# A token mixer, masked attention product and routed FFN on one Trainium2 core: x rows of tile 3 loaded earlier, attention weights split in halves of 512, prologue order rewritten

## Chip, cores and metric

The kernel runs on one core of one Trainium2 chip. The metric is the device time of one execution in microseconds (us). Three timed executions of the kernel before gave 526.52, 526.66 and 527.02 us (median 526.66). The profiled execution is another one, with a time of its own.

## What is computed

The input `x` is (16, 128, 64, 2): 16 channels c, 128 heads h, 64 complex states n. The output is (16, 128, 1024).

```python
# 1. token mixer (S4D): K[c,h,l] = Re( sum_n W'[c,h,n] * exp(dt_Lambda[h,n] * l) ),  l = 0..1023
dt_Lambda = exp(log_dt) * Lambda
W' = W * (exp(dt_Lambda) - 1) * reciprocal((exp(dt_Lambda * 1024) - 1) * Lambda)
h = einsum('chn,hnl->chl', W', exp(dt_Lambda * pos)).real
# 2. attention product with a block mask (32 x 32 blocks, kept where the mask's sum is over 0)
h = h + layernorm(h) @ (weight * block_mask).T          # weight 1024 x 1024
# 3. FFN with a sparsemax router over 8 experts of rank 16
y = layernorm(h)
h = h + y @ W_base.T + b_base + sum_e sparsemax(y @ W_router.T + b_router)[e] * (y @ lora_A[e]) @ lora_B[e]
```

## The kernel before

The 16 x 128 = 2048 rows of length 1024 are worked on in 16 tiles of 128 rows (8 heads x 16 channels). For each tile `t`:

- ScalarE and VectorE build two small tables (`sines`, `exponentials`, `phases`, `decay_b`, `v_factors`), VectorE multiplies them with x into `v_sb` (`table_v`), and `b_sb` is built on GpSimd in the prologue and on VectorE in the loop (`table_b`). TensorE multiplies the two per head (`k_transposed`), which gives K transposed in `turnp`.
- `k_high` (ScalarE) and `k_low` (VectorE) split it into a high and a low fp32r part, the stationary operand of the attention product. `k_turn` (VectorE) turns it back; SyncE stores it to `rows_out` in four transfers and loads it again as rows `h1` (`k_rows`), of which `k_sum` and `k_deviation` take the statistics.
- `attention(t, k)`, k = 0..7, is the product with the attention weights, in three passes (high x high, low weights, low data) over both halves of 512 columns: 6 matmuls a chunk. `attention_residual` scales it and adds `h1`.
- `h2_transposes`, `h2_high`, `h2_low` prepare the FFN's operand; `lora_router` gives expert activations and logits, `gates` the sparsemax, `gated_transpose`/`gated_high`/`gated_low` their split operand, `base(t, k)` the base product, `experts` the expert product, `result` the output rows; GpSimd's `add_bias` prepares the rows that `result` adds to.

The rows of x come into one buffer `xn`, which `load_x(t)` (SyncE) fills and `x_rows_twice(t)` (ScalarE) copies to `xd`; `x_transposes(t)` (TensorE) turns it into the PSUM bank `xps` that `table_v(t)` reads. There is one `xn` and one `xps`, so `load_x(t)` waits for `x_rows_twice(t-1)`, that one for `x_transposes(t-1)`, and `x_transposes(t)` for `table_v(t-1)`.

The loop over tiles 2 to 15 has two products per step: attention of tile t, base of tile t-1. Ahead of it stands a **prologue**, an order of calls written out by hand on each engine, in which tiles 0 to 3 start and the weights are prepared:

- Attention weights, 8 row blocks j: `mask_sums(j)` (VectorE) and `block_sums(j)` (TensorE) give the block mask, `wa_mask(j)` (VectorE) applies it, `wa_centre(j)` (ScalarE for j < 6, GpSimd for 6 and 7) takes the row's mean off, `wa_transposes(j)` (TensorE) transposes it in two halves i = 2j, 2j+1 of 512 columns into the two halves of `acc_b`, `wa_copies(j)` (ScalarE) rounds them to `wa_hi`, and `wa_lo` is the difference: from PSUM by VectorE (`wa_lows`), or for j = 1, 3, 5 (`BY_POOL`) by GpSimd from a copy in SBUF that `wa_copies(j)` makes as well. A half of `acc_b` is used again when both have read it.
- Base weights, 16 halves i: `wb_half(i)` (TensorE), `wb_highs(i)` (ScalarE), `wb_lows(i)` (VectorE), through the same two halves of `acc_b`.
- `first_attention(n, [k])` is the attention product of tile 0, first for the half n = 0 of the columns (weights j = 0..3), then for n = 1.
- `q_arguments`, `q_tanh`, `q_sines`, `reciprocal_of_tanh`, GpSimd's `parameters` and `reciprocal_of_norm` give the factor of W': round 0 for the heads of tiles 0 and 1, round 1 for all others.

The product of tile 0 (base and experts) closes the prologue: `base(0, 0)` waits for all 16 `wb_high` and `wb_low`, `gated_transpose(0)` for `gates(0, 0)`, `experts()` for `gated_low(0)`.

Each engine works through its own list in order. SyncE's list is: all mask and attention weight rows, `load_x(1)`, base weights, LoRA A, `load_x(2)`, `k_rows(0)`, `k_rows(1)`, a wait for `q_ready` 2 (the end of `parameters(1)`), LoRA B (into `lb_raw`), the bias, `load_x(3)`, `k_rows(2)`, `load_x(4)`. The waits of its `k_rows` are:

```python
sp.wait_ge(kt_turned, t + 1)                 # k_turn(t)
if at(t, 1):
    sp.wait_ge(h2_ready, t)                  # attention_residual(0, 0)
...                                          # four stores to rows_out
sp.wait_ge(k_out, (t + 1) * 16 * Q)          # they have landed
```

Of the kernel before, what the change touches and what calls it, by code (L numbers as in the profile page):

```python
# [21 lines left out]
P = 128  # L22
# [47 lines left out]
def build_vit_tower(nc, x, log_dt, lam, w_attn, mask, w_base, b_base, w_router, b_router, lora_a, lora_b,  # L70
# [4 lines left out]
    with ExitStack() as ctx:  # L75
# [138 lines left out]
        def half_bank(i):  # L214
            return acc_b[:, (i % 2) * HALF:(i % 2 + 1) * HALF]
# [91 lines left out]
        def _(sp):  # L307
# [28 lines left out]
            k_rows(0)  # L336
            k_rows(1)
# [3 lines left out]
            load_x(3)  # L341
# [26 lines left out]
        def _(pe):  # L368
# [16 lines left out]
            def wa_transposes(j):  # L385
                if j < CENTRE_LAST:
                    pe.wait_ge(wa_centred, j + 1)
                else:
                    pe.wait_ge(wa_centred_last, j + 1 - CENTRE_LAST)
                for i in (2 * j, 2 * j + 1):  # L390
                    if i >= 2:
                        pe.wait_ge(wa_high, i - 1)
                        if (i - 2) // 2 in BY_POOL:
                            pe.wait_ge(wa_copied, raws(i - 1))
                        else:
                            pe.wait_ge(wa_low_direct, i - 1 - raws(i - 1))
# [146 lines left out]
            block_sums(7)
            pe.wait_ge(kt_lo, 1)
            wa_rows_ready(NWT // 2)
            first_attention(0, [0])
            wa_transposes(4)
# [3 lines left out]
            x_transposes(1)  # L551
            wa_transposes(5)
            wa_transposes(6)
            wa_transposes(7)
            first_attention(0, [4])
            first_attention(0, [5])
            first_attention(0, [6])
            wb_half(0)
            wb_half(1)
            first_attention(0, [7])  # L560
# [55 lines left out]
            experts()  # L616

# [20 lines left out]
        def _(act):  # L638
# [129 lines left out]

            q_tanh(0)
            q_sines(0)  # L770
            sines(0)
            wa_centre(0)
            exponentials(0)
            wa_centre(1)
            wa_centre(2)
            wa_copies(0)
            x_rows_twice(0)
# [589 lines left out]
```

## Time and profile before

| | before |
|---|---|
| timed executions | 526.66 us median (526.52 to 527.02) |
| profiled execution, its time | 525.62 us |
| profiled execution, its span (first to last instruction) | 523.8 us |
| mean granted TensorE clock | 0.984 |
| busy in the span: PE, PEld, DVE, ACT, POOL | 92%, 78%, 78%, 50%, 23% |
| `experts()` of tile 0 ends, the loop's first instruction starts | 110.5 us |

PE is TensorE's matmul, PEld its weight load, DVE VectorE, ACT ScalarE, POOL GpSimd, SP SyncE. All times of the trace are counted from the start of the span. The part ahead of 110.5 us is the prologue; the rest are the 14 steps of the loop and the tail.

### The profile page before, as it was taken

Reading aid. Unit: us, or ns where it says so; the run is one execution under the profiler, and the core shown is the slowest. Engines: PE = TensorE matmul, PEld = TensorE weight load, DVE = VectorE, ACT = ScalarE, POOL = GpSimd, SP = SyncE. Lnnn points to the kernel's source line nnn. Section 1 sums busy time; section 2 is a strip of 40 time slices with the busy share of each in tenths; the row PEclk is TensorE's granted clock in tenths of the full one; section 3 lists DMA queues with packets and bytes.
Section 4 is the critical chain, followed back from the end, with each engine's and each line's share of the span. In section 5 each row is a group of like instructions: output and inputs, shape, how many; then the busy total and the mean of one; then the engine's idle time right before and its main releaser. Section 6 shows DMA issues by size and latency. Waiting matters only on the chain.

```text
span 523.8 us, 7437 instructions
## 1 busy us (share of the span) xinstructions
PE 480.9 (92%) x2467; PEld 407.9 (78%) x2467; DVE 410.9 (78%) x866; ACT 262.4 (50%) x477; POOL 122.1 (23%) x106
## 2 busy tenths in 40 slices
PE   0548977989999999999999999999999999999995
PEld 0446766878888888888888888888888888888884
DVE  7998985998988889888888878887889888854241
ACT  2687976467363636455464646362635446232200
POOL 0574694440201103030303030201203030303020
PEclk9997988999999999999999999999999999999998
DMA  8994113031312121221203040312121120303011
GB/s 286 403 320 68 37 42 126 1 94 37 92 37 81 44 80 45 49 76 40 85 8 117 0 111 14 90 35 80 45 80 47 42 79 18 103 20 102 1 40 40
DMA packets 28764, 40.83 MB, mean 78 GB/s; under 512 B 10760, under 2 KB 21192, under 8 KB 28744
## 3 DMA queue, kind: packets, MB, share of 16 engines
q1 hardware_dynamic: 28368, 40.49, 25.5%
q8 instruction: 10, 0.16, 0.1%
q10 hardware_dynamic: 376, 0.10, 0.1%
q14 instruction: 10, 0.08, 0.0%
HBM read 23.80 MB, written 16.78 MB: 77 GB/s over the span
## 4 chain that ended last, share of the span: by engine, by line
PE 83%; ACT 5%; DVE 4%; POOL 3%; DMA 3%; issue 1%; SPq 0%; DVEq 0%; POOLq 0%
PE acc_b L455 36%; PE acc_a L455 31%; PE turnp L439 5%; PE small L479 4%; PE turnp L448 3%; DMA xn<-in_x 2%; PE small L481 1%; PE acc_b L399 1%; ACT wa_hi L661 1%; ACT wa_raw L655 1%; ACT wb_hi L670 1%; PE xps L429 1%; POOL wr L937 0%; ACT wa_raw L664 0%; PE acc_b L420 0%
## 5 line engine op out<-in xcount | busy, mean ns | idle before, releaser
L946 POOL TENSOR_TENSOR h<-h,st 128x1024 f32<-128x1024 f32 x16 | 30.3, 1894 | 328.6 <-PE turnp L448 321.5
L455 PE MATMUL acc_a<-wa_hi,x_hi 128*128 128x512 f32 x256 | 84.2, 405 | 2.1 <-POOL wa_lo L925 1.6
L455 PE MATMUL acc_b<-wb_hi,x_hi 128*128 128x512 f32 x256 | 83.9, 404 | 0.0
L455 PE MATMUL acc_a<-wa_lo,x_hi 128*128 128x512 f32 x256 | 81.4, 394 | 0.0
L455 PE MATMUL acc_a<-wa_hi,x_lo 128*128 128x512 f32 x256 | 81.0, 393 | 0.0
L455 PE MATMUL acc_b<-wb_lo,x_hi 128*128 128x512 f32 x256 | 80.6, 391 | 0.0
L455 PE MATMUL acc_b<-wb_hi,x_lo 128*128 128x512 f32 x256 | 80.5, 391 | 0.0
L455 PEld LDWEIGHTS acc_a<-wa_lo,x_hi 128*128 128x128 f32 x256 | 48.9, 191 | 10.2
L455 PEld LDWEIGHTS acc_a<-wa_hi,x_lo 128*128 128x128 f32 x256 | 48.5, 190 | 10.4
L742 ACT ACTIVATE x_hi<-turnp 128x1024 fp32r<-128x1024 f32 x16 | 16.4, 1023 | 80.0 <-PE turnp L448 80.0
L455 PEld LDWEIGHTS acc_a<-wa_hi,x_hi 128*128 128x128 f32 x256 | 47.7, 192 | 11.0 <-DVE x_lo L1150 1.7
L455 PEld LDWEIGHTS acc_b<-wb_hi,x_lo 128*128 128x128 f32 x256 | 48.1, 188 | 10.4
L455 PEld LDWEIGHTS acc_b<-wb_lo,x_hi 128*128 128x128 f32 x256 | 48.1, 188 | 10.3
L455 PEld LDWEIGHTS acc_b<-wb_hi,x_hi 128*128 128x128 f32 x256 | 44.9, 189 | 8.2
L1216 DVE SCALAR_TENSOR_TENSOR h<-acc_b,st,h 128x1024 f32<-128x1024 f32 (+1 forms) x17 | 20.7, 1220 | 25.5 <-PE acc_b L455 25.5
L949 POOL TENSOR_TENSOR h<-h,bias 128x1024 f32<-128x1024 f32 x16 | 39.4, 2465 | 1.3
L748 ACT ACTIVATE hw_hi<-small 128x128 fp32r<-128x128 f32 x16 | 4.4, 278 | 64.6 <-PE small L487 64.6
L1150 DVE TENSOR_TENSOR x_lo<-turnp,x_hi 128x1024 fp32r<-128x1024 f32 x16 | 19.6, 1224 | 21.9 <-ACT x_hi L707 21.9
L439 PEld LDWEIGHTS turnp<-v_sb,b_sb 128*128 128x128 f32 x256 | 31.3, 195 | 1.8 <-issue 0.8
L479 PE MATMUL small<-wr,x_hi 128*128 128x272 f32 x128 | 32.1, 338 | 0.0
L439 PE MATMUL turnp<-v_sb,b_sb 128*128 128x128 f32 x256 | 31.9, 279 | 0.2 <-issue 0.2
L682 ACT ACTIVATE er_t<-er_t 128x256 f32<-128x256 f32 x15 | 6.3, 418 | 48.4 <-DVE er_t L1073 48.4
(200 smaller groups left out, 940.2 us busy)
## 6 DMA issues: line engine op xcount, KB each, us to landing
h<-rows_out SPq DMA_DIRECT2D x16, 512.0 KB, 3.3
out<-h SPq DMA_DIRECT2D x15, 512.0 KB
rows_out<-b_sb SPq DMA_DIRECT2D x56, 128.0 KB, 2.3
mask_raw<-in_L_attn_mask SPq DMA_DIRECT2D x8, 512.0 KB, 10.0
wa_raw<-in_L_attn_weight SPq DMA_DIRECT2D x8, 512.0 KB, 10.7
wb_raw<-in_L_ffn_W_base SPq DMA_DIRECT2D x8, 512.0 KB, 8.8
rows_out<-tmp SPq DMA_DIRECT2D x8, 128.0 KB, 2.3
xn<-in_x SPq DMA_DIRECT2D x15, 64.0 KB
```

The source lines that it names most:

```text
L399: mm = pe.transpose(half_bank(i)[:, k * P:(k + 1) * P], every_eighth, ident)
L429: mm = pe.transpose(xps[:, r * P:(r + 1) * P], xd[:, r, :, :].rearrange("p d n -> p (d n)"), ident)
L439: mm = pe.matmul(kt_pairs[:, h // HG, :, h % HG * C:(h % HG + 1) * C], b_sb[:, h, :, :].rearrange("p x y -> p (x y)"), v_sb[:, h, :, :], s ...
L448: mm = pe.transpose(turnp[:, k * P:(k + 1) * P], h2[par][:, k * P:(k + 1) * P], ident)
L455: return pe.matmul(cols, a, rows, start=first, stop=last)
L479: pe.matmul(small[:, 0:2 * CAT], x_hi[:, k, :], wr[:, k, :, :].rearrange("p s n -> p (s n)"), start=k == 0, stop=False)
L682: act.activation(er_of(t), er_of(t), ACT.Exp).then_inc(tab_exp, 1)
L742: act.activation(x2_of(t)[0][:, :, :].rearrange("p k n -> p (k n)"), turnp[:, :], ACT.Copy)\
L946: pool.tensor_tensor(h2[par][:, :], h2[par][:, :], st2[:, par, 1:2].to_broadcast([P, L]), ALU.subtract)\
L949: pool.tensor_tensor(h2[par][:, :], h2[par][:, :], bias[:, :], ALU.add).then_inc(bias_added, 1)
L1150: dve.tensor_tensor(by_pair(lo), kt_pairs, by_pair(hi).bitcast(F), ALU.subtract).then_inc(kt_lo, 1)
L1216: dve.scalar_tensor_tensor(h, acc_b[:, cols], st2[:, par, 4:5], h, ALU.mult, ALU.add).then_inc(out_ready, 1)
```

## The change

1. SyncE: `load_x(3)` moves up, from behind LoRA B and the bias to right behind `k_rows(0)`.
2. `wa_transposes(j)` and `wa_copies(j)`, which did both halves of a block, become `wa_half(i)` (TensorE), `wa_highs(i)` and `wa_raws(j)` (ScalarE), and `wa_lows` of VectorE takes a half i. The waits of each half are as before. `wa_raws(j)` stands behind both `wa_highs` of its block.
3. The lists of TensorE, ScalarE and VectorE in the prologue are in another order; the instructions are the same ones. GpSimd's list is unchanged. The tables of numbers that follow the calls (which tile, which half) are unchanged.

```diff
             k_rows(0)
+            load_x(3)
             k_rows(1)
             sp.wait_ge(q_ready, len(ROUNDS))
             sp.dma_start(lb_raw[:, :], lora_b.rearrange("e r l -> (e r) l")).then_inc(lorb_in, 16)
             sp.dma_start(bias[:, :], b_base.partition_broadcast(P)).then_inc(bias_in, 16)
-            load_x(3)
             k_rows(2)
             load_x(4)
...
-            def wa_transposes(j):
+            def wa_half(i):
+                j = i // 2
                 if j < CENTRE_LAST:
                     pe.wait_ge(wa_centred, j + 1)
                 else:
                     pe.wait_ge(wa_centred_last, j + 1 - CENTRE_LAST)
...
-            def wa_copies(j):
-
+            def wa_highs(i):
+
+                act.wait_ge(wa_t, i + 1)
+                act.activation(half_of(wa_hi, i), half_bank(i), ACT.Copy).then_inc(wa_high, 1)
+
+            def wa_raws(j):
+
+                act.wait_ge(wa_t, 2 * j + 2)
                 for i in (2 * j, 2 * j + 1):
-                    act.wait_ge(wa_t, i + 1)
-                    act.activation(half_of(wa_hi, i), half_bank(i), ACT.Copy).then_inc(wa_high, 1)
-                if j in BY_POOL:
-                    for i in (2 * j, 2 * j + 1):
-                        act.activation(raw_half(i), half_bank(i), ACT.Copy).then_inc(wa_copied, 1)
+                    act.activation(raw_half(i), half_bank(i), ACT.Copy).then_inc(wa_copied, 1)
...
-            def wa_lows(j):
-
-                dve.wait_ge(wa_t, 2 * j + 2)
-                for i in (2 * j, 2 * j + 1):
-                    dve.wait_ge(wa_high, i + 1)
-                    dve.tensor_tensor(half_of(wa_lo, i), half_bank(i), half_of(wa_hi, i).bitcast(F), ALU.subtract)\
-                        .then_inc(wa_low_direct, 1)
+            def wa_lows(i):
+
+                dve.wait_ge(wa_t, i // 2 * 2 + 2)
+                dve.wait_ge(wa_high, i + 1)
+                dve.tensor_tensor(half_of(wa_lo, i), half_bank(i), half_of(wa_hi, i).bitcast(F), ALU.subtract)\
+                    .then_inc(wa_low_direct, 1)
```

The lists after the change, by calls (TensorE, from the fourth block sum on; ScalarE and VectorE where the prediction speaks of them; `hi`/`lo`/`raw` are `wa_highs`, `wa_lows`, `wa_raws`):

```
TensorE: wa_half 0,1 | router transpose | block_sums 3,4 | x_transposes 0 | block_sums 5 | wa_half 2,3,4,5 |
  block_sums 6 | k_transposed 0 | wa_half 6 | x_transposes 1 | wa_half 7 | block_sums 7 | wa_half 8,9 |
  first_attention 0: k 0-3 | wa_half 10-15 | first_attention 0: k 4-7 | wb_half 0,1 | first_attention 1: k 0-4 |
  wb_half 2,3 | k 5 | x_transposes 2 | k_transposed 1 | k 6,7 | wb_half 4-9 | attention(1,0) |
  h2_transposes 0 | attention(1,1) | wb_half 10,11 | attention(1,2),(1,3) | wb_half 12,13 |
  attention(1,4),(1,5) | wb_half 14,15 | lora_router 0 | attention(1,6),(1,7) | k_transposed 2 |
  base(0,0) to (0,6) | gated_transpose 0 | base(0,7) | experts | x_transposes 3
ScalarE: ... exponentials 0 | centre 2 | hi 2,3 | raw 1 | centre 3,4 | x_rows_twice 1 | hi 4,5,6 | k_high 0 |
  hi 7 | raw 3 | hi 8,9 | exponentials 1 | centre 5 | sines 1 | hi 10,11 | raw 5 | x_rows_twice 2 |
  hi 12-15 | q_tanh 1 | wb_highs 0,1 | k_sum 0, k_deviation 0 | wb_highs 2,3 | router/LoRA copy | q_sines 1 |
  wb_highs 4 | k_high 1 | ... | wb_highs 10,11 | sines 2 | k_sum 1 | wb_highs 12-15 | x_rows_twice 3 |
  k_deviation 1 | exponentials 3 | k_high 2 | h2_centre 1 | LoRA B copy | gated_high 0 | sines 3
VectorE: ... lo 4,5 | phases 1 | wa_mask 5,6 | k_low 0 | wa_mask 7 | lo 8,9 | router_columns |
  q_arguments 1 | decay_b 1 | k_turn 0 | lo 12,13 | v_factors 1 | lo 14,15 | table_v 1 | wb_lows 0,1 | ... |
  wb_lows 10,11 | h2_reciprocal 0 | v_factors 2 | decay_b 2 | wb_lows 12,13 | table_v 2 | wb_lows 14,15 |
  h1_reciprocal 1 | attention_residual 1 | phases 3 | gates 0 | k_low 2 | k_turn 2 | gated_low 0 |
  result 0 | v_factors 3 | table_v 3
```

Three places, row by row. SyncE, behind the rows of tile 0 (L319 and L322 are the rows of K of one tile, L311 is `load_x`):

```order
 L319 DMA rows_out<-tmp 32x4x256 x4
 L322 DMA h<-rows_out 128x1024
+L311 DMA xn<-in_x 128x1x128
 L319 DMA rows_out<-tmp 32x4x256 x4
 L322 DMA h<-rows_out 128x1024
-L339 DMA lb_raw<-in_L_ffn_lora_B 128x1024
-L340 DMA bias<-in_L_ffn_b_base 128x1024
-L311 DMA xn<-in_x 128x1x128
+L340 DMA lb_raw<-in_L_ffn_lora_B 128x1024
+L341 DMA bias<-in_L_ffn_b_base 128x1024
```

The load of the x rows passes the rows of tile 1 and the two loads that wait for `parameters(1)`.

VectorE around `k_low(0)` (L1150), before: `wa_mask(5)` and `wa_mask(6)` (L1044) stand on either side of it, then round 1 of the arguments (L1013 to L1018) and the two lows of block 4 (L1052):

```order
L1044 SCALAR_TENSOR_TENSOR wa_raw,wa_sum<-acc_a,wa_raw 128x1024
L1150 TENSOR_TENSOR x_lo<-turnp,x_hi 128x4x8x32
L1044 SCALAR_TENSOR_TENSOR wa_raw,wa_sum<-small,wa_raw 128x1024
```

The same place after the change (L1170 is `k_low(0)`, L1065 `wa_mask`, L1072 the lows of halves 8 and 9):

```order
L1065 SCALAR_TENSOR_TENSOR wa_raw,wa_sum<-acc_a,wa_raw 128x1024
L1065 SCALAR_TENSOR_TENSOR wa_raw,wa_sum<-small,wa_raw 128x1024
L1170 TENSOR_TENSOR x_lo<-turnp,x_hi 128x4x8x32
L1065 SCALAR_TENSOR_TENSOR wa_raw,wa_sum<-acc_a,wa_raw 128x1024
L1072 TENSOR_TENSOR wa_lo<-acc_b,wa_hi 128x512 x2
```

`wa_mask(6)` now stands ahead of `k_low(0)`, and `wa_mask(7)` and block 4 right behind it.

VectorE behind the gates of tile 0, before: `k_low(2)` (L1150), `gated_low(0)` (L1210), `k_turn(2)` (L1156), `v_factors(3)` (L1094 to L1100), `result(0, 0)` (L1216):

```order
L1150 TENSOR_TENSOR x_lo<-turnp,x_hi 128x4x8x32
L1210 TENSOR_TENSOR hw_lo<-small,hw_hi 128x128
L1156 STREAM_TRANSPOSE b_sb<-turnp 128x4x8x32
L1094 TENSOR_TENSOR xy<-xy,er_t 128x128
L1096 TENSOR_TENSOR t<-xy,qr 128x128
L1097 TENSOR_TENSOR t<-xy,qi 128x128
L1099 TENSOR_TENSOR u<-t 128x64
L1100 TENSOR_TENSOR u<-t 128x64
L1216 SCALAR_TENSOR_TENSOR h_0<-acc_b,st,h_0 128x1024
```

The same after the change, with the line numbers of the changed kernel (L1176 is `k_turn(2)`, L1230 `gated_low(0)`, L1236 `result(0, 0)`):

```order
L1170 TENSOR_TENSOR x_lo<-turnp,x_hi 128x4x8x32
L1176 STREAM_TRANSPOSE b_sb<-turnp 128x4x8x32
L1230 TENSOR_TENSOR hw_lo<-small,hw_hi 128x128
L1236 SCALAR_TENSOR_TENSOR h_0<-acc_b,st,h_0 128x1024
L1114 TENSOR_TENSOR xy<-xy,er_t 128x128
```

`k_turn(2)` has passed `gated_low(0)`, and `v_factors(3)` follows `result(0, 0)`.

## Rows read from the trace of the kernel before

**Rows 1.** By stretch: length, busy PE, PEld, DVE, ACT, POOL, granted clock, DMA share, GB/s

```profile
26.00:39.00 13.00, 6.18 (x38) 5.63 (x37) 12.86 (x20) 11.03 (x23) 9.37 (x5) 1.00 0.99 325
...
78.00:91.00 13.00, 9.44 (x50) 8.15 (x49) 7.47 (x16) 7.88 (x19) 6.62 (x5) 0.87 0.36 127
...
140.00:523.00 383.00, 377.88 (x1938) 320.45 (x1936) 289.30 (x622) 173.18 (x315) 60.12 (x28) 1.00 0.20 57
```

**Rows 2.** Waits between 0 and 112 us: in total, times, longest

```profile
PE acc_b L420 <- ACT wb_hi L670: 3.6, 1, 3.6
...
PE small L487 <- DVE hw_sb L1197: 1.8, 1, 1.8
```

**Rows 3.** Timeline of SyncE's queue: start us, us, engine line op

```profile
78.46 0.35 SPq L339 DMA_DIRECT2D lb_raw<-in_L_ffn_lora_B  x1
...
79.34 0.64 SPq L311 DMA_DIRECT2D xn<-in_x  x1
```

**Rows 4.** Timeline of ScalarE: start us, us, ..., [idle before <-releaser]

```profile
35.49 1.11 ACT L664 ACTIVATE wa_raw<-acc_b 128x512 f32<-128x512 f32 x2
...
85.31 0.52 ACT L677 ACTIVATE xd<-xn 128x128 f32<-128x128 f32 x2 [5.02 <-DMA xn<-in_x]
```

**Rows 5.** Timeline of TensorE

```profile
39.28 0.77 PE L455 MATMUL acc_a<-wa_hi,x_hi 128*128 128x512 f32 x1 [1.57 <-POOL wa_lo L925]
...
74.34 1.04 PE L448 MATMUL turnp<-kst,h 128*128 128x128 f32 x8
...
87.14 1.94 PE L420 MATMUL acc_b<-kst,wb_raw 128*128 128x128 f32 x8 [3.56 <-ACT wb_hi L670]
...
96.00 0.71 PE L455 MATMUL acc_b<-wb_hi,x_hi 128*128 128x512 f32 x2
...
101.53 0.62 PE L455 MATMUL acc_b<-wb_hi,x_hi 128*128 128x512 f32 x2
...
122.65 2.02 PE L439 MATMUL turnp<-v_sb,b_sb 128*128 128x128 f32 x16 [0.18 <-issue]
```

**Rows 6.** Timeline of VectorE in the prologue

```profile
37.09 1.22 DVE L1150 TENSOR_TENSOR x_lo<-turnp,x_hi 128x1024 fp32r<-128x1024 f32 x1
38.23 1.22 DVE L1044 SCALAR_TENSOR_TENSOR wa_raw<-small,wa_raw 128x1024 f32<-128x1024 f32 x1
...
62.37 2.13 DVE L1168 TENSOR_TENSOR st<-st 128x1 f32<-128x1 f32 x1
...
93.89 1.28 DVE L1174 SCALAR_TENSOR_TENSOR h<-acc_a,st,h 128x1024 f32<-128x1024 f32 x1 [0.70 <-issue]
...
99.43 2.17 DVE L1191 TENSOR_TENSOR gate<-gate,gs 128x64 f32<-128x64 f32 x1
...
103.63 2.21 DVE L1196 TENSOR_SCALAR gs<-gs,tau 128x8 f32<-128x8 f32 x1
105.87 0.29 DVE L1197 TENSOR_TENSOR hw_sb<-cat,gs 128x128 f32<-128x128 f32 x1
...
107.41 2.19 DVE L1156 STREAM_TRANSPOSE b_sb<-turnp 128x1024 f32<-128x1024 f32 x1
```

**Rows 7.** VectorE in the first step of the loop, the same gate operation

```profile
131.18 0.22 DVE L1191 TENSOR_TENSOR gate<-gate,gs 128x64 f32<-128x64 f32 x1
```

**Rows 8.** Timeline of GpSimd in the prologue

```profile
36.67 2.35 POOL L925 TENSOR_TENSOR wa_lo<-wa_raw,wa_hi 128x1024 fp32r<-128x1024 f32 x1 [3.55 <-ACT wa_raw L664]
...
61.95 2.53 POOL L937 TENSOR_TENSOR wr<-wr_raw,wr 128x1088 fp32r<-128x1088 f32 x1 [4.20 <-ACT wr L806]
...
86.25 2.37 POOL L912 TENSOR_TENSOR b_sb<-b_sb,h 128x1024 f32<-128x1024 f32 x1
99.12 2.40 POOL L941 TENSOR_TENSOR lb_lo<-lb_raw,lb_hi 128x1024 fp32r<-128x1024 f32 x1 [10.51 <-ACT lb_hi L831]
101.48 1.89 POOL L946 TENSOR_TENSOR h<-h,st 128x1024 f32<-128x1024 f32 x1
103.45 2.36 POOL L949 TENSOR_TENSOR h<-h,bias 128x1024 f32<-128x1024 f32 x1
```

More of the change, by code:

```diff
@@ L550, in _ @@
             first_attention(0, [3])
[L551 to L554, printed above, removed]
+            wa_half(10)
+            wa_half(11)
+            wa_half(12)
+            wa_half(13)
+            wa_half(14)
+            wa_half(15)
             first_attention(0, [4])
@@ L589, in _ @@
             attention(1, 3)
+            wb_half(12)
+            wb_half(13)
+            attention(1, 4)
+            attention(1, 5)
+            wb_half(14)
+            wb_half(15)
             pe.wait_ge(h2t_lo, 1)
@@ L616, in _ @@
             experts()
+            x_transposes(3)
             steps(pe, step)
@@ L767, in _ @@
             act.dma_start(rt_stage, w_router.rearrange("e (k p) -> (e k) p", p=P)).then_inc(rt_in, 16)
+            x_rows_twice(0)
             q_tanh(0)
[L770 to L777, printed above, removed]
-            wa_centre(3)
-            x_rows_twice(1)
             act.wait_ge(ldt_in, 16)
@@ L782, in _ @@
             act.wait_ge(consts_in, 16)
-            wa_copies(1)
+            q_sines(0)
+            wa_centre(0)
+            wa_centre(1)
+            sines(0)
+            wa_highs(0)
+            wa_highs(1)
+            exponentials(0)
+            wa_centre(2)
+            wa_highs(2)
+            wa_highs(3)
+            wa_raws(1)
+            wa_centre(3)
             wa_centre(4)
-            wa_copies(2)
+            x_rows_twice(1)
+            wa_highs(4)
+            wa_highs(5)
+            wa_highs(6)
             k_high(0)
-            wa_copies(3)
+            wa_highs(7)
+            wa_raws(3)
+            wa_highs(8)
+            wa_highs(9)
+            exponentials(1)
+            wa_centre(5)
             sines(1)
-            exponentials(1)
-            wa_copies(4)
-            wa_centre(5)
-            wa_copies(5)
+            wa_highs(10)
+            wa_highs(11)
+            wa_raws(5)
             x_rows_twice(2)
+            wa_highs(12)
+            wa_highs(13)
+            wa_highs(14)
+            wa_highs(15)
             q_tanh(1)
-            wa_copies(6)
-            wa_copies(7)
-            q_sines(1)
             wb_highs(0)
@@ L806, in _ @@
             act.activation(wr[:, :, 0, :], cat_raw, ACT.Copy).then_inc(cat_hi, 1)
+            q_sines(1)
+            wb_highs(4)
             k_high(1)
-            wb_highs(4)
             wb_highs(5)
@@ L812, in _ @@
             wb_highs(7)
+            h2_centre(0, 0)
             wb_highs(8)
             wb_highs(9)
-            h2_centre(0, 0)
             h2_deviation(0, 0)
             h2_high(0)
+            wb_highs(10)
+            wb_highs(11)
             sines(2)
-            wb_highs(10)
-            x_rows_twice(3)
-            wb_highs(11)
+            k_sum(1)
             wb_highs(12)
-            k_sum(1)
-            k_deviation(1)
             wb_highs(13)
@@ L827, in _ @@
             wb_highs(15)
+            x_rows_twice(3)
+            k_deviation(1)
             exponentials(3)
+            k_high(2)
             h2_centre(1, 1)
@@ L1328, in _ @@
             k_low(2)
+            k_turn(2)
             gated_low(0)
-            k_turn(2)
-            v_factors(3)
             dve.wait_ge(ffn_ready, 1)
             result(0, 0)
+            v_factors(3)
             table_v(3)
```

122 lines of the change are left out of this document (62 added, 60 removed).

## Prediction

> **What bounds the kernel now.** I read the granted clock and the busy time by stretch first. In the loop TensorE is busy 377.9 of 383 us at full clock, so only the prologue and the first step can give anything [rows 1]. The prologue falls in two parts. From 26 to 39 us VectorE works 12.86 of 13 us while TensorE works 6.18: this part is bound by VectorE's list, and TensorE's first attention product starts at 39.28, right behind `k_low(0)` (37.09 plus 1.14) and GpSimd's `wa_lo` of block 3, which ends at 39.03 [rows 1, 5, 6, 8]. From 78 to 91 us TensorE is busy 9.44 of 13 us, at a mean clock of 0.87 of full speed, and nobody else is full: that is waiting, not work [rows 1].
>
> The wait that ends last there is in ScalarE's timeline: `x_rows_twice(3)` stands idle 5.02 us until 85.31 for the x rows of tile 3 [rows 4]. SyncE issued them at 79.34, behind LoRA B at 78.46, which waits for the end of `parameters(1)` [rows 3]. Behind it on ScalarE is `wb_highs(11)`, and TensorE's `wb_half(13)` starts at 87.14 after 3.56 us of idle, eight transposes in 1.94 us where eight of `h2_transposes` took 1.04 [rows 2, 5]. The half-speed stretch is the 1.2 GHz level, after the idle. The other end of this part is the gates of tile 0, for which TensorE waits 1.8 us [rows 2]. The prologue closes at 110.5 us.
>
> **Part by part.** No instruction is added or taken away, so I followed each list with the durations of the rows. A VectorE pass over 128x1024 costs 1.14 us from start to start [rows 6], a half of 512 0.6 on VectorE and 0.5 on ScalarE, an attention or base chunk of six matmuls 1.38 at full clock (from 96.00 to 101.53 there are four) [rows 5]. The results:
>
> *Up to the first attention: later by 1.9 us.* VectorE has `wa_mask(6)` ahead of `k_low(0)`, 1.14 us [rows 6], and two short waits of 0.5 (for GpSimd's norm) and 0.8 (for `wa_highs(4)`, which now stands behind `wa_centre(3)`, `(4)` and `x_rows_twice(1)`); 0.25 of idle goes. `k_low(0)` ends at 40.5 instead of 38.3. ScalarE's raw copies of block 3 end at 38.7 instead of 36.6 [rows 4], so GpSimd's `wa_lo`, 2.35 us, ends at 41.1 instead of 39.0 [rows 8]. TensorE starts at 41.2 instead of 39.3.
>
> *41 to 76 us: about level.* What TensorE lacks there it has done before: `wa_half(8)` and `(9)`, 1.9 us at half clock, no longer stand among the chunks. `wa_mask(7)` is done 5 us earlier, which takes the late centring by GpSimd off the path of blocks 6 and 7. VectorE finishes `table_v(1)` at about 56.2, as before, `k_turn(0)` 1.2 later. Then `h1` lands 1.2 us later, ScalarE's `k_deviation(0)` ends about 1.0 later, and `q_sines(1)` with its table load (1.97 us) is now behind it instead of ahead. The wait in front of `wb_half(6)` stays. I get the end of `h2_transposes(0)` at 75.9 against 75.2 to 75.4 before [rows 5].
>
> One collision I can't place: VectorE's first operation of `reciprocal_of_tanh(1)` would start at 62.9, GpSimd's `cat_lo` at about the same moment. In the trace a 128x1 operation of VectorE that began with this GpSimd operation in progress (61.95, 2.53 us) took 2.13 us, from 62.37 until that was over [rows 6, 8]. If GpSimd is first, `wb_lows(4)` is 1.7 us late and 1.1 us of it reach the end; if not, nothing. Between 0 and 1.1 I take 0.5.
>
> *76 us to the end of attention: earlier by 4.9 us.* The x load now goes out right behind the rows of tile 0, near 53 us, when `x_rows_twice(2)` is done; even 6 us of transfer end 25 us before `x_rows_twice(3)`. So the 5.02 and the 3.56 us go, and with them the half-clock transposes (0.9) and chunks (about 0.7) behind them. In their place TensorE's list runs nearly closed: 75.9, plus `wb_half(10..13)` 1.8, four chunks 5.5, `wb_half(14,15)` 1.2 with a short wait, `lora_router` 1.85, two chunks 2.75. Attention of tile 1 ends at 88.9; before it was 93.8, since `attention_residual(1,1)` starts at 93.89 [rows 6]. `k_transposed(2)` adds 1.8, and base starts at 90.7 instead of 96.0 [rows 5]. What is late next is GpSimd: `parameters(1)` starts at 65.5 instead of 64.5 and takes 14.0 us, then `v_factors(2)`, `decay_b(2)` and 6.2 us of `table_b(2)` end at 88.8, against 88.6 before [rows 8]. It gave 5 us of slack before and gives none now: a further gain ahead of this point is worth nothing.
>
> *From there to the gates: 0.4 later.* The gates' end stood 12.3 us behind the end of attention (105.87 plus 0.29 against 93.8) [rows 6]. Three gate operations are stretched by the three GpSimd operations beside them, among them one of 2.17 us that takes 0.22 in the loop; they end as those end [rows 6 to 8]. Their start comes from ScalarE's copy of LoRA B, and `k_high(2)` now stands ahead of it. I take the same distance plus 0.4: 101.7.
>
> *Gates to the end of `experts`: 0.65 later.* Before, TensorE's own chunks filled the time behind the gates: 110.5 minus 106.15 is 4.35. Now `gated_low(0)` stands behind `k_low(2)` (1.14) and `k_turn(2)` (2.19) [rows 6], 0.3 more for itself, and the expert product 1.36: 5.0. TensorE arrives at `gated_transpose(0)` near 100.3, and has only `base(0,7)` to fill 3.6 us: a new wait of about 2 us at `experts`.
>
> *First step: 0.4 later.* `k_transposed(3)` waits 0.18 us at 122.65, so VectorE's chain to `table_b(3)` is already even with TensorE [rows 5]. `v_factors(3)`, 1.2 us, is now inside that chain, behind `result(0, 0)`, which in turn starts 0.6 earlier relative to the end of experts; `x_transposes(3)` (0.2) moves from one place of TensorE's list to another. Net 0.4. Behind it the loop has slack on VectorE (289 of 383 us) [rows 1].
>
> The sum: -4.9 + 0.4 + 0.65 + 0.4 + 0.5 = -2.95 us. Of the profiled execution's 525.6 us that leaves 522.7. The median of the runs shown is 1.0 us above that execution, so I forecast 523.7 us.
>
> **Rivals.** *Forecast case* (the x wait goes, the new waits at `experts` and in the first step take part of it): gain 1.2 to 4.8, chance 0.60.
>
> *The gates slip through*, gain 5.2, 521.5 us, chance 0.18. The first stretched operation (99.43) began 0.3 us after GpSimd's (99.12) [rows 6, 8]; by my times it now begins 0.4 us before, and is done. Then only two are held, and the gates end at 99.5 instead of 101.7. Against it: the last gate operation would then stand beside GpSimd's third one, and rows show it only after that was over. The Trainium skill (SBUF — State Buffer, "Who interferes with whom") says that a VectorE instruction with two SBUF inputs contends with a GpSimd one that reads SBUF, and that the loser waits for the whole instruction; by that rule the last operation, both of whose inputs are in SBUF, is held too and the end is 101.7 again. The trace agrees on the first of them: 2.17 against 0.22 us.
>
> *The late start stays*, gain 1.0, 525.7 us: no change, chance 0.13. The 1.9 us at the first attention aren't made up by the work done ahead, because TensorE meets new waits at `wa_half(12)` and `(14)` (ScalarE's `sines(1)`, 3.3 us with its table load, stands ahead of `wa_highs(10)`). -2.95 + 1.9 = -1.05. The same result stands for the case that the x rows were hidden after all. For it: the walk rests on a dozen near ties; against it: VectorE's list, which binds, has no new work.
>
> *GpSimd's parameter chain becomes the path*, slower, 528.7 us, chance 0.09. `q_sines(1)` is behind `k_deviation(0)` and the router copy, so `parameters(1)` moves with `h1`, which moves with `k_turn(0)`. Each us that it starts behind 65.5 is one us at `k_transposed(2)`, at `attention_residual(1,1)` and at the gates. The kernel turns slower when it starts 3 us later, behind 68.5; at 70.5 (`h1` landing late, and the collision at 62.9 delaying what the chain waits for) it is -2.95 + 5 = +2.05. Against it: GpSimd is free from 58 us on, and the rows of `h1` have the DMA engines nearly alone.
>
> **How the numbers follow.** A measurement of this kernel can tell about 0.2% (1.05 us) from no change. Faster by more: 0.60 + 0.18 = 0.78; within it 0.13; slower 0.09. The range takes the forecast case, the slipping gates with 2 us of error on my walk, and the late start: 519.2 to 526.2.
>
> **What would show it.** Right: `x_rows_twice(3)` without idle; base of tile 0 starting near 90.7; first attention near 41.2; idle of about 2 us in front of the expert product; `table_b(2)` of GpSimd ending within 0.5 us of `k_transposed(2)`; 0.5 us of idle at `k_transposed(3)`. Wrong: base starting later than 94, `parameters(1)` starting after 68, or a first attention that starts as early as before.

## The result, and the profile after

Over eight runs of each, the changed kernel takes 525.21 us (median; 524.42 to 525.60), the kernel before 526.84 us (526.10 to 527.62). The ratio is 0.9968 [0.9957, 0.9978]: 1.6 us faster, half of the 3.1 us that the forecast of 523.7 us meant.

| | before | after |
|---|---|---|
| median us | 526.84 | 525.21 |
| profiled execution / span, us | 525.62 / 523.8 | 524.96 / 523.1 |
| VectorE, ScalarE, GpSimd busy, after | | 411.4 (79%), 262.8 (50%), 122.0 (23%) |

The two profiled executions differ by only 0.7 us, because before's lies 1.2 us below its median and after's 0.25 below. The windows of the kernel after answer to [rows 1] (length, busy PE, PEld, DVE, ACT, POOL, granted clock, DMA share, GB/s):

```profile
26.00:39.00 13.00, 9.51 (x48) 9.00 (x49) 12.11 (x21) 9.02 (x17) 6.93 (x4) 0.98 0.98 321
65.00:78.00 13.00, 8.66 (x37) 7.00 (x37) 10.70 (x14) 10.40 (x16) 12.02 (x25) 0.74 0.17 42
78.00:91.00 13.00, 12.93 (x77) 10.91 (x75) 11.01 (x24) 11.09 (x23) 7.11 (x6) 1.00 0.36 122
...
140.00:523.00 383.00, 377.21 (x1934) 319.72 (x1932) 288.83 (x622) 173.26 (x315) 59.69 (x28) 1.00 0.20 56
```

The hole between 78 and 91 us is closed: TensorE works 12.93 us of 13 at full clock, where it worked 9.44. The loop is as it was. The stretch ahead of the hole has become worse: 8.66 us of work at a granted clock of 0.74, where the same window of the kernel before reads

```profile
65.00:78.00 13.00, 9.82 (x52) 8.26 (x53) 11.66 (x16) 9.59 (x15) 11.94 (x25) 0.87 0.17 42
```

TensorE's timeline of the kernel after answers to [rows 5]:

```profile
41.66 0.77 PE L455 MATMUL acc_a<-wa_hi,x_hi 128*128 128x512 f32 x1 [0.64 <-ACT wa_hi L668]
...
67.57 0.63 PE L420 MATMUL acc_b<-kst,wb_raw 128*128 128x128 f32 x4 [2.52 <-ACT wb_hi L680]
69.37 1.08 PE L420 MATMUL acc_b<-kst,wb_raw 128*128 128x128 f32 x4 [1.17 <-ACT wb_hi L680]
71.10 1.94 PE L420 MATMUL acc_b<-kst,wb_raw 128*128 128x128 f32 x8 [0.64 <-ACT wb_hi L680]
...
75.40 1.40 PE L448 MATMUL turnp<-kst,h 128*128 128x128 f32 x8
...
90.72 0.61 PE L455 MATMUL acc_a<-wa_hi,x_lo 128*128 128x512 f32 x2
92.11 2.02 PE L439 MATMUL turnp<-v_sb,b_sb 128*128 128x128 f32 x16 [0.77 <-issue]
93.89 0.70 PE L455 MATMUL acc_b<-wb_hi,x_hi 128*128 128x512 f32 x2
...
105.62 0.70 PE L455 MATMUL acc_b<-lb_hi,hw_hi 128*128 128x512 f32 x2 [0.42 <-DVE hw_lo L1230]
107.08 0.38 PE L429 MATMUL xps<-kst,xd 128*128 128x128 f32 x2
...
121.98 2.02 PE L439 MATMUL turnp<-v_sb,b_sb 128*128 128x128 f32 x16 [2.76 <-issue]
```

The reader sees four things: the first attention product at 41.66; three waits ahead of `wb_half(6)` to `(8)`, with transposes at half clock behind them (eight in 1.94 us, granted clock 0.50); the base product of tile 0 at 93.89, only 2.1 us earlier than before; and a new wait of 2.76 us for `k_transposed(3)` in the first step, where 0.18 stood. ScalarE's row that answers to [rows 4] has no idle:

```profile
87.23 0.53 ACT L687 ACTIVATE xd<-xn 128x128 f32<-128x128 f32 x2
```

VectorE's timeline of the kernel after, where [rows 6] were read:

```profile
63.24 2.10 DVE L1045 TENSOR_SCALAR lb_raw<-bias 128x224 f32<-128x224 f32 x1
...
92.16 1.28 DVE L1194 SCALAR_TENSOR_TENSOR h<-acc_a,st,h 128x1024 f32<-128x1024 f32 x1
...
97.07 0.22 DVE L1211 TENSOR_TENSOR gate<-gate,gs 128x64 f32<-128x64 f32 x1
...
97.64 2.28 DVE L1214 SCALAR_TENSOR_TENSOR gs<-gs 128x8 f32<-128x8 f32 x1
...
100.16 1.63 DVE L1216 TENSOR_SCALAR gs<-gs,tau 128x8 f32<-128x8 f32 x1
101.82 0.29 DVE L1217 TENSOR_TENSOR hw_sb<-cat,gs 128x128 f32<-128x128 f32 x1
...
112.21 3.42 DVE L1144 TENSOR_TENSOR v_sb<-tmp,v_sb 128x1024 f32<-128x1024 f32 x1
```

And GpSimd's, where [rows 8] were read:

```profile
62.69 2.52 POOL L958 TENSOR_TENSOR wr<-wr_raw,wr 128x1088 fp32r<-128x1088 f32 x1 [3.73 <-ACT wr L826]
...
84.85 1.94 POOL L930 TENSOR_TENSOR b_sb<-pp,qq 128x1024 f32<-128x1024 f32 x1 [5.74 <-DVE qq L1152]
...
88.76 3.25 POOL L933 TENSOR_TENSOR b_sb<-b_sb,h 128x1024 f32<-128x1024 f32 x1
...
97.50 2.40 POOL L962 TENSOR_TENSOR lb_lo<-lb_raw,lb_hi 128x1024 fp32r<-128x1024 f32 x1 [5.49 <-ACT lb_hi L853]
99.86 1.90 POOL L967 TENSOR_TENSOR h<-h,st 128x1024 f32<-128x1024 f32 x1
101.84 2.54 POOL L970 TENSOR_TENSOR h<-h,bias 128x1024 f32<-128x1024 f32 x1
...
112.15 2.40 POOL L970 TENSOR_TENSOR h<-h,bias 128x1024 f32<-128x1024 f32 x1
```

Read in pairs. At 62.69 GpSimd's `cat_lo` begins, and VectorE's first operation of `reciprocal_of_tanh(1)` (63.24) is not done before it ends, at 65.2. The kernel before has a hold of the same length beside the same GpSimd operation, at a neighbouring operation of VectorE (62.37, 2.13 us [rows 6]). At 112.15 `add_bias(1)`'s second operation begins, 0.06 us ahead of the last operation of `table_v(3)` (L1144), which then takes 3.42 us instead of 1.23. In the kernel before the same pair stood the other way round: VectorE's began at 114.85 and took 1.23, GpSimd's at 114.88 and took 3.47.

So most of the time won by the end of the experts (their end, read as the start of `x_transposes(3)`: 107.08 against 110.52, 3.4 us) is gone at `k_transposed(3)` (121.98 against 122.65, 0.7 us).

### The profile page after: what moved, and what is told of

The parts are those of the page before. It is cut to its first block, busy times and chain, and to the rows that moved or that the text cites. A ratio compares the mean times of both kernels' runs of the same rounds, so it can differ in the third digit from the quotient of the medians.

```text
span 523.1 us, 7442 instructions
## 1 busy us (share of the span) xinstructions
PE 482.6 (92%) x2467; PEld 408.1 (78%) x2467; DVE 411.4 (79%) x866; ACT 262.8 (50%) x477; POOL 122.0 (23%) x106
## 4 chain that ended last, share of the span: by engine, by line
PE 84%; DVE 7%; ACT 3%; issue 3%; POOL 1%; DMA 0%; DVEq 0%; POOLq 0%; ACTq 0%
PE acc_b L455 36%; PE acc_a L455 32%; PE turnp L439 5%; PE small L479 4%; PE turnp L448 3%; PE small L481 1%; PE acc_b L420 1%; PE acc_b L399 1%; ACT wa_hi L668 1%; ACT wb_hi L680 1%; PE xps L429 1%; DVE wa_lo L1072 0%; DVE wb_lo L1078 0%; DVE gs L1214 0%; DVE mask_sum L1056 0%
## 5 line engine op out<-in xcount | busy, mean ns | idle before, releaser
L1236 DVE SCALAR_TENSOR_TENSOR h<-acc_b,st,h 128x1024 f32<-128x1024 f32 (+1 forms) x17 | 20.7, 1221 | 27.3 <-PE acc_b L455 27.3
L1170 DVE TENSOR_TENSOR x_lo<-turnp,x_hi 128x1024 fp32r<-128x1024 f32 x16 | 19.6, 1224 | 22.0 <-ACT x_hi L717 22.0
```

What stands on the lines that cost most here:

```text
L1170: dve.tensor_tensor(by_pair(lo), kt_pairs, by_pair(hi).bitcast(F), ALU.subtract).then_inc(kt_lo, 1)
L1236: dve.scalar_tensor_tensor(h, acc_b[:, cols], st2[:, par, 4:5], h, ALU.mult, ALU.add).then_inc(out_ready, 1)
```

## The experiments

Each kernel was timed over five rounds; medians of before measured beside it are given as (before ...). The comparison of the traces left two theories on the x load: that it brings about 4 us and the new order gives them back (`b1_x_alone`), and that the new order has made it worthless (`a1_x_late`).

**The x load alone taken back, and the x load alone.** `a1_x_late` is the changed kernel with

```diff
             k_rows(0)
-            load_x(3)
...
+            load_x(3)
             k_rows(2)
```

behind LoRA B and the bias, and `b1_x_alone` the kernel before with the opposite edit.

> The changed kernel with load_x(3) put back behind the bias, all else as changed. Theory (the new order has made the early load worthless): x_rows_twice(3) now stands behind wb_highs(15), at 87.2 us in the changed kernel's trace; a load issued at 80.0 lands near 86, so ScalarE waits for nothing, and the time is that of the changed kernel, 525.2 us within 0.5. Rival (my prediction's step: the load is what took the 5 us wait away): the wait comes back, at least 3 us slower than the changed kernel, 528 us.

> The kernel before with load_x(3) moved up behind k_rows(0), nothing else. Theory (the early load is the gain, the rest of the new order costs): x_rows_twice(3) starts at about 80.3 instead of 85.3, base of tile 0 near 91 instead of 96.0, then bound by GpSimd's table_b(2), which ends at 88.6; 4 to 5 us faster than before, about 522 us, faster than the whole change. Rival (the gain is capped by GpSimd's chain and by TensorE's waits as in the changed kernel): base starts near 94 and the gain is 1.5 us, 525.2 us.

`a1_x_late`: 525.31 us (before 527.12), 0.9971 [0.9958, 0.9984], the same as the changed kernel. Its SyncE and ScalarE, one row of each:

```profile
78.92 0.64 SPq L311 DMA_DIRECT2D xn<-in_x  x1
...
85.97 0.52 ACT L687 ACTIVATE xd<-xn 128x128 f32<-128x128 f32 x2
```

The rows are issued as late as before (78.92 against 79.34) and nobody waits for them: in the new order of ScalarE `x_rows_twice(3)` stands behind `sines(2)`, `k_sum(1)` and `wb_highs(12..15)`, and 7 us have passed. The early load is worth nothing beside the new order, as the recorded theory of this run had it.

`b1_x_alone`: 526.23 us (before 527.12), 0.9982 [0.9964, 0.9999]: 0.9 us, with an interval that ends just short of no change; its theory (4 to 5 us) and its rival (1.5 us) were both too high. From the start of `h2_transposes(0)` to base its trace is 3.1 us shorter than that of the kernel before. (The profiled execution took 527.83 us, 1.6 above this run's median, so it shows where the gain goes and not how large it is.) TensorE then has nothing to do before the gates are done:

```profile
106.03 0.33 PE L487 MATMUL small<-kst,hw_sb 128*128 128x128 f32 x1 [2.06 <-DVE hw_sb L1197]
...
108.01 1.06 PE L455 MATMUL acc_b<-wb_hi,x_hi 128*128 128x512 f32 x2
```

Behind the 2.06 us of idle four groups of base matmuls run at the 1.2 GHz level (1.06 us a pair instead of 0.62, granted clock 0.50 from 108 to 110), and `k_transposed(3)` waits 1.00: here too VectorE's last operation of `table_v(3)` began with GpSimd's in progress (115.72 behind 115.03) and took 2.80 us instead of 1.23. The theory that the load alone brings 4 us fell: each of the two edits removes the same wait. The load buys 0.9 us in the old order and none in the new.

**The tie at `table_v(3)`.** `a2_pool_wait` makes GpSimd's second operation of `add_bias` wait for the V table of two tiles ahead, `a3_v_first` moves `v_factors(3)` forward on VectorE, as it was before the change:

```diff
                 pool.wait_ge(mean_added, t + 1)
+                if not isinstance(t, int) or t + 3 <= TILES:
+                    pool.wait_ge(v_ready, t + 3)
```

```diff
+            v_factors(3)
             dve.wait_ge(ffn_ready, 1)
             result(0, 0)
-            v_factors(3)
```

> The changed kernel, where the second operation of GpSimd's add_bias(t) also waits for v_ready of tile t+2, so that it can't begin ahead of the last operation of table_v(3). Theory (in the changed kernel that operation of VectorE took 3.42 us instead of 1.23 because GpSimd's had begun 0.06 us before): it takes 1.23 again, the idle before k_transposed(3) falls from 2.76 to about 0.6, and the kernel is up to 2.2 us faster than the changed one in a profile, 523.0 to 525 us in time. Rival (the wait comes from v_factors(3) behind result(0,0)): no change, 525.2 us, idle 2.5 us.

> The changed kernel with v_factors(3) again ahead of result(0,0). Theory (sines(3) ends at 107.28, as late as the experts, so the order of the two makes no difference by itself): table_v(3) starts within 0.2 us of 109.82, time 525.2 within 0.5 us unless the collision with GpSimd falls otherwise. Rival (the 1.2 us of v_factors(3) are what TensorE waits for): 1.2 us faster, 524.0 us.

`a2_pool_wait`: 523.12 us (before 527.12), 0.9932 [0.9912, 0.9953]. `a3_v_first`: 522.72 us (before 527.12), 0.992 [0.990, 0.994]. Both lie 1.9 to 2.5 us below the changed kernel's ratio, with intervals clear of its own. In the first, VectorE and GpSimd around L1144 (now L1146) are:

```profile
111.34 1.23 DVE L1146 TENSOR_TENSOR v_sb<-tmp,v_sb 128x1024 f32<-128x1024 f32 x1
...
112.65 2.41 POOL L972 TENSOR_TENSOR h<-h,bias 128x1024 f32<-128x1024 f32 x1 [1.50 <-DVE v_sb L1146]
...
119.37 2.02 PE L439 MATMUL turnp<-v_sb,b_sb 128*128 128x128 f32 x16 [1.01 <-issue]
```

VectorE is free, `k_transposed(3)` waits 1.01 instead of 2.76. In the second nothing forbids the collision, and it falls the other way by 0.02 us, which the recorded text had left open:

```profile
112.00 1.23 DVE L1144 TENSOR_TENSOR v_sb<-tmp,v_sb 128x1024 f32<-128x1024 f32 x1
...
112.02 3.48 POOL L970 TENSOR_TENSOR h<-h,bias 128x1024 f32<-128x1024 f32 x1
...
119.81 2.02 PE L439 MATMUL turnp<-v_sb,b_sb 128*128 128x128 f32 x16 [0.69 <-issue]
```

`v_factors(3)` moved `table_v(3)` by 0.2 us in these profiles (109.62 against 109.82); that was enough to turn the tie, and the turn is worth ten times the move. That the lost tie costs the changed kernel about 2 us is shown by two different edits.

**The collision at 63 us.** `c1_cat_behind` lets GpSimd's `cat_lo` follow `parameters(1)` instead of preceding it:

```diff
-            pool.wait_ge(cat_hi, 1)
-            pool.tensor_tensor(wr[:, :, 1, :], cat_raw, wr[:, :, 0, :].bitcast(F), ALU.subtract).then_inc(cat_lo, 1)
             parameters(1)
+            pool.wait_ge(cat_hi, 1)
+            pool.tensor_tensor(wr[:, :, 1, :], cat_raw, wr[:, :, 0, :].bitcast(F), ALU.subtract).then_inc(cat_lo, 1)
```

> The changed kernel with GpSimd's low part of the router and LoRA A columns (cat_lo) behind parameters(1) instead of ahead. Theory (in the changed kernel the first operation of reciprocal_of_tanh(1) took 2.10 us instead of 0.2 because that GpSimd operation had begun before it, and TensorE then lost 2.5, 1.2 and 0.6 us in front of wb_half(6), (7) and (8) and ran them and attention(1,0) at half clock): the operation takes 0.3, wb_lows(4) ends 1.8 us earlier, base of tile 0 starts at least 1 us earlier than the 93.9 of the changed kernel, and the time falls by 1 to 2 us, to about 523.7. Rival (GpSimd's chain to table_b(2) decides): base starts at 93.5 to 94 and the time stays at 525.2.

524.08 us (before 527.13), 0.9945 [0.9931, 0.9959]: 1.2 us below the changed kernel by the ratios, though the two intervals just touch. Its TensorE, to be held against the three waits above, and its VectorE:

```profile
65.83 0.63 PE L420 MATMUL acc_b<-kst,wb_raw 128*128 128x128 f32 x4 [1.02 <-ACT wb_hi L680]
67.64 0.63 PE L420 MATMUL acc_b<-kst,wb_raw 128*128 128x128 f32 x4 [1.18 <-issue]
69.46 1.94 PE L420 MATMUL acc_b<-kst,wb_raw 128*128 128x128 f32 x8 [1.19 <-ACT wb_hi L680]
73.04 1.03 PE L448 MATMUL turnp<-kst,h 128*128 128x128 f32 x8
...
89.76 2.02 PE L439 MATMUL turnp<-v_sb,b_sb 128*128 128x128 f32 x16 [0.76 <-issue]
...
119.60 3.41 PE L439 MATMUL turnp<-v_sb,b_sb 128*128 128x128 f32 x16 [2.72 <-issue]
```

```profile
63.03 0.27 DVE L1045 TENSOR_SCALAR lb_raw<-bias 128x224 f32<-128x224 f32 x1
...
78.70 2.07 DVE L1188 TENSOR_TENSOR st<-st 128x1 f32<-128x1 f32 x1
...
109.83 3.43 DVE L1144 TENSOR_TENSOR v_sb<-tmp,v_sb 128x1024 f32<-128x1024 f32 x1
```

`k_transposed(2)` starts at 89.76 instead of 92.11. The held operation of VectorE is only moved: a 128x1 operation of `h2_reciprocal(0)` now stands beside `cat_lo` and takes 2.07 us, where it matters less. The window from 65 to 78 us reads 9.80 us of TensorE at 0.87 again, as in the kernel before. The tie of `table_v(3)` is still lost, which costs no more than in the changed kernel: `k_transposed(3)` starts 2.4 us earlier (119.60 against 121.98) behind the same idle (2.72 against 2.76). But it then takes 3.41 us instead of 2.02, at a granted clock of 0.50 from 120 to 123 where the changed kernel's was 1.00, and that is 1.4 of the 2.4 us. Whether the executions that were not profiled lost it in the same way is not known.

The kernel before has this hold as well (62.37, 2.13 us), so it is no loss of the change but one that both kernels carry.

**The three together.** `c2_three` has `a2`, `a3` and `c1` in one kernel.

> The changed kernel with v_factors(3) ahead of result(0,0), the wait of add_bias for v_ready, and cat_lo behind parameters(1). Theory (the wait in the first step and the block at reciprocal_of_tanh(1) are separate, and the second is worth 1 to 2 us): 521.3 to 522.3 us, faster than either a2 (523.1) or a3 (522.7). Rival (a2 and a3 already have all there is): 522.7 to 523.1 us.

521.39 us (before 527.13), 0.9899 [0.9883, 0.9916], as its theory had it. In the changed kernel the two collisions together cost 0.9968 minus 0.9899, 0.69% or 3.6 us; only the tie of `table_v(3)` came with the change.

**An earlier start.** The first attention had moved from 39.28 to 41.66 us, and TensorE waits 3.50 us for a block sum of `wa` that stands ahead of `wa_half(2)`. `c3_halves` puts the two halves ahead of the sum; `c4_five` is `c2_three` with this and with `gated_low(0)` ahead of `k_turn(2)`:

```diff
-            block_sums(5)
             wa_half(2)
             wa_half(3)
+            block_sums(5)
...
+            gated_low(0)
             k_turn(2)
-            gated_low(0)
```

> The changed kernel with wa_half(2) and wa_half(3) ahead of block_sums(5) on TensorE, where block_sums(5) waits for wa_mask(3) until 26.2 us and ScalarE for wa_half(2) until 27.7. Theory (the late start of the first attention costs at the end): ScalarE's copies of block 1 come 2 to 5 us earlier, the first attention starts near 40 us instead of 41.7, and about half of that is left at the end, 524.5 us. Rival (the waits behind it absorb an earlier start): the first attention starts earlier and the time stays within 0.5 us of 525.2.

> All of it together: c2_three, c3_halves, and gated_low(0) ahead of k_turn(2). Theory (gated_low(0) costs only the 0.4 us that TensorE idles in front of the expert product): 0.3 to 1 us faster than c2_three, 520.5 to 521.7 us. Rival (my prediction's step, that it costs 2 us): 2 us faster than c2_three, under 520 us.

`c3_halves`: 526.54 us (before 527.13), 0.9986 [0.9975, 0.9997], about 1 us slower than the changed kernel by the ratios, with intervals that just meet; theory and rival both miss. The transposes come earlier, and the hole comes behind them:

```profile
31.89 3.78 PE L439 MATMUL turnp<-v_sb,b_sb 128*128 128x128 f32 x16 [2.29 <-DVE v_sb L1144]
35.46 1.06 PE L399 MATMUL acc_b<-kst,wa_raw 128*128 128x128 f32 x4
...
42.23 0.76 PE L455 MATMUL acc_a<-wa_hi,x_hi 128*128 128x512 f32 x1 [1.87 <-POOL wa_lo L946]
```

In the changed kernel the same four transposes took 0.60 us; here they take 1.06, half the pace. The granted clock reads 1.00 throughout that stretch (31 to 38 us) in both traces, and `k_transposed(0)` ahead of them took 3.61 and 3.78 us in the two, so these rows do not show that the clock is the reason. The first attention starts at 42.23, later than 41.66. `k_transposed(0)` starts at 31.88 in the one and 31.89 in the other, since it waits for VectorE. Where the 1 us at the end comes from stays open: `k_transposed(2)` starts only 0.4 us later than in the changed kernel, and 1.1 us of the difference of the two profiles is `k_transposed(3)`, which took 3.09 us instead of 2.02.

`c4_five`: 521.36 us (before 527.13), 0.9898 [0.9882, 0.9914], the same as `c2_three`; here too theory and rival both expected a gain. The wait at the expert product goes and reappears at `k_transposed(3)` (1.40 instead of 0.83). Beside the collisions, then, neither of these waits is worth anything by itself.

**The same cures on the kernel before.** `d1_before_wait` is the kernel before with the wait of `a2`; `d2_before_three` has that wait, `load_x(3)` early and `cat_lo` behind `parameters(1)`. They ask what the new order is worth once the collisions are out of both.

> The kernel before with only the wait of GpSimd's add_bias for v_ready of tile t+2. In the trace of before VectorE's last operation of table_v(3) began 0.03 us ahead of GpSimd's and took 1.23 us. Theory (before mostly wins this tie, the new order turned it round): 526.5 to 527.2 us, no change against before. Rival (it is lost in many executions of before too): 1 us faster or more, under 526 us.

> The kernel before with load_x(3) early, the wait of add_bias, and cat_lo behind parameters(1): the old order of the three engines with the collisions taken away. Theory (the new order by itself is worth something once nothing collides): 523 to 525 us, at least 1.5 us slower than c2_three (521.4), which has the new order. Rival (all that the new order does is to shift collisions): 521.0 to 522.0 us, the same as c2_three.

`d1_before_wait`: 527.68 us (before 527.53), 1.0008 [0.9991, 1.0024], no difference: before wins that tie anyway. `d2_before_three`: 524.53 us (before 527.53), 0.9945 [0.9931, 0.9960]. Against `c2_three` (0.9899) the new order is worth 0.46%, 2.4 us. The trace of `d2_before_three` also loses a tie one table earlier,

```profile
87.22 3.43 DVE L1126 TENSOR_TENSOR v_sb<-tmp,v_sb 128x1024 f32<-128x1024 f32 x1
```

so part of the 2.4 us may be that tie and not the order; this was not taken apart. Against `b1_x_alone` (0.9982) the two cures bring 0.37%, 1.9 us, in the old order; how much of it is the hold at 63 us and how much the tie that `b1_x_alone` loses in its trace is open.

**A version that beats both.** `d3_sines` is `c2_three` with ScalarE's `sines(3)` ahead of `gated_high(0)`:

```diff
+            sines(3)
             gated_high(0)
-            sines(3)
```

> c2_three with sines(3) ahead of gated_high(0) on ScalarE, which there waits 6 us for the gates. Theory (VectorE's chain from sines(3) over v_factors(3), result, table_v(3) and table_b(3) is what k_transposed(3) waits for, 0.83 us in c2_three): v_factors(3) is done before the expert product ends, the idle goes, 0.6 to 1.0 us faster, 520.5 us. Rival (the time is lost again in the steps of the loop): within 0.3 us of 521.4.

520.71 us (before 527.53), 0.9876 [0.9859, 0.9892]: 1.24% faster than the kernel before, 4.8 us better than the changed kernel by the ratios. Against `c2_three` it is 0.7 us by the medians, and the intervals overlap, so that last step is likely but not shown. `k_transposed(3)` starts at 117.86 without idle; the wait of GpSimd for the V table is 1.85 us and costs nothing there.

```profile
110.95 2.41 POOL L972 TENSOR_TENSOR h<-h,bias 128x1024 f32<-128x1024 f32 x1 [1.85 <-DVE v_sb L1146]
...
117.86 1.95 PE L439 MATMUL turnp<-v_sb,b_sb 128*128 128x128 f32 x16
```

## Why the prediction was right or wrong

Faster, and inside the range; the gain was half of what was forecast. By the steps of the sum, against before's profiled execution:

| step | predicted | measured |
|---|---|---|
| first attention | 41.2 | 41.66 |
| end of `h2_transposes(0)` | 75.9 (+0.5 for the collision, added apart) | 76.56 |
| end of attention on TensorE | -4.9, at 88.9 | -2.5: 91.33 against 93.80 |
| `attention_residual(1,1)` behind it | at once | 92.16 against 93.89: -1.7 |
| start of base | 90.7, from 96.00 | 93.89 |
| `attention_residual(1,1)` to the gates' end | +0.4 | 9.95 against 12.27: -2.3 |
| gates to the end of `experts` | +0.65 (5.0) | +0.62 (4.97) |
| first step | +0.4 | +2.8 |

**First attention, right.** VectorE's extra `wa_mask(6)` and the later raw copies put it 2.4 us later instead of 1.9: GpSimd's `wa_lo` of block 3 ended at 41.40 where I had 41.1. That this needn't cost the end held too, in the sense that TensorE was at `wb_half(6)` in time to wait there. An attempt to start it earlier (`c3_halves`) failed.

**41 to 76 us: the collision, mis-sized.** I had it as undecided between 0 and 1.1 us and took 0.5. It happened: GpSimd began 0.55 us before VectorE. `h2_transposes(0)` ended 0.7 us later than my 75.9, of which the term covers 0.5. But the price of a hold was too low: without it `c1_cat_behind` starts `k_transposed(2)` 2.3 us earlier, and 1.2 us reach the median. With the held operation the three waits for `wb_high` come to 4.3 us (2.52, 1.17 and 0.64; 3.4 without it), and more of what follows, up to 76 us, runs at half clock, `h2_transposes(0)` among it (1.40 us instead of 1.03). That lowered clock was priced nowhere in the sum.

**"-4.9 until the end of attention", wrong: -2.5.** The wait for the x rows went, as said, and TensorE's list runs closed from 78 to 91 us, as said. What failed is the walk along that list. From 75.9 to 88.9 it adds up "four chunks" and "two chunks", but the changed list has seven chunks behind `h2_transposes(0)`, `attention(1,1)` to `(1,7)`; six is the number of the kernel before, where `attention(1,1)` stood ahead of the transposes. One chunk, 1.4 us by my own price, is missing. Measured, this stretch runs from 76.56 to 91.33, 14.8 us where I had 13.0: the missing chunk and 0.4 us more. With the chunk in it the sum would have been -1.57 us and the forecast 525.1 us; that it then meets the measured 525.21 would be luck too, since other terms missed by more.

The second part is "what is late next is GpSimd ... it gave 5 us of slack before and gives none now". The path it names is right and its size is not: TensorE was through with attention at 91.33 and `k_transposed(2)` started at 92.11, 0.1 us behind the end of `table_b(2)` (92.01 instead of my 88.8). So of the 3.2 us by which base is late against 90.7, 2.4 are TensorE's own list and 0.8 are GpSimd's. `parameters(1)` started at 65.16, within 0.4 us of the 65.5 I gave. But `table_b(2)` began only at 84.85, released by VectorE's `decay_b(2)`, which waits for ScalarE's `sines(2)`, which stands behind `wb_highs(10)` and so behind TensorE's `wb_half(10)` (78.02), the first item behind the chunk I left out. And its last operation took 3.25 us instead of 2.37, because VectorE's L1144 of tile 2 was in progress. `c1_cat_behind` moves all of this together: attention ends at 89.00 and `k_transposed(2)` starts at 89.76.

**The credit for the x load, wrong in its place.** The text put the removed waits of 5.02 and 3.56 us down to the load's new place in the queue. `a1_x_late` shows that the new order, in which `x_rows_twice(3)` stands behind `wb_highs(12..15)`, removes them without the early load, and `b1_x_alone` that the load by itself brings 0.9 us. I had asked what the load passes in SyncE's queue and not whether ScalarE's new order had made its lateness harmless.

**The gates, wrong and on the good side.** The mechanism of the rival of the slipping gates came true, though not its time of 521.5 us: the operation at 97.07 took 0.22 us, before GpSimd's first at 97.50, and only two operations were held (2.28 and 1.63). The last one began 0.02 us before GpSimd's third, and GpSimd's took 2.54 instead of 2.36. The weighing against that rival expected the last operation to be held; it was not, because VectorE was first. The Trainium skill (SBUF — State Buffer, "Who interferes with whom") has the rule that whoever issues first keeps the shared ports, stated for whole instructions; I had used its sentence on who contends and not the one on order, and the trace agrees with both (3.42 and 3.47 us for the two losers of the same pair).

**The experts, right by chance.** Their end was forecast for 107.15 and came at 107.08: 3.2 us of gain too much on the way to `attention_residual(1,1)` and 2.7 us too little on the gates nearly cancel, with the 0.5 us of the collision that I added apart. The gates-to-experts distance was right (4.97 us), the wait of 2 us was 0.42, because TensorE reached `gated_transpose(0)` only at 103.54 and not at 100.3.

**"First step: 0.4 later", wrong: 2.8.** This is the step that halved the gain. I listed the moved `v_factors(3)` and `x_transposes(3)` with their durations, and left out who else works at that moment. `add_bias(1)` of GpSimd had begun 0.03 us behind VectorE's last table operation in the kernel before; a shift of 0.1 us turns it and costs 2.2 us on the path to `k_transposed(3)`; the other 0.6 is near the 0.4 that I had for the moved calls. `a2_pool_wait`, `a3_v_first` and `c2_three` show it from three sides. The row 114.88 with its 3.47 us was in the trace of before and would have told it.

## What to carry to other kernels

Where VectorE and GpSimd share work on a tile, look in the trace for pairs in which one of the two is much longer than its own usual duration: such a pair is a tie, the next edit may turn it, and a semaphore wait on the engine that has slack fixes the order (here it cost nothing). Add up a stretch from the list of calls as it stands after the change: here one chunk of 1.4 us went missing because the count was that of the old order. Test each part of a change alone: a transfer's early start and a later use of it removed the same wait here, and only one of them was worth its line. A transfer that is brought forward may only move the hole, and the clock can fall behind the new one, as in `b1_x_alone`.

## What the runs showed of the hardware

- The order of two starts 0.02 to 0.06 us apart decided which engine was held, for the same two instructions: VectorE's took 1.23 us or 3.42, GpSimd's 2.4 or 3.48. In either order the later one ended about when both, one after the other, would have (112.15 + 2.40, then 1.08 more up to 115.63).
- Operations of tiny size are held until about the end of the GpSimd operation, as large ones are: 128x1 took 2.07 us beside one of 2.52, 128x8 took 2.28 beside one of 2.40. One with a single tensor as input was held too (L1045, 128x224: 2.10 us against 0.27).
- TensorE's clock fell behind some waits and not behind others of the same length. Behind 2.06 us of idle in `b1_x_alone` the granted clock was 1.00 for one more us and then 0.50: pairs of 512-column matmuls in 1.06 us instead of 0.62. Behind 2.72 us at `k_transposed(3)` in `c1_cat_behind` it was 0.50 and the product took 3.41 us; behind 2.76 us at the same place in the changed kernel it was 1.00 and the product took 2.02.
- Half the pace is not always seen in the granted clock: between 32 and 37 us `k_transposed(0)` took 3.61 us in the changed kernel and 3.78 in `c3_halves`, at a recorded clock of 1.00 and with about 400 GB/s of transfers for most of that time. The cause was not tested.
- Seventeen runs of the kernel before in the last series lie between 525.5 and 529.5 us, four of `c2_three` between 520.8 and 522.1. That the removed ties are the cause was not tested: `d1_before_wait`, with only the wait of `add_bias` added, still spreads from 526.0 to 529.1.
